# GpSimd's scatters one pass later, the keys' scaling ahead of the first addition, and the state's second scaling ahead of the last three additions

## The reference

```python
mixed = conv4(einsum('bth,ch->btc', layernorm(x), qkv_w))   # causal, one filter per channel
q, k, v = split(mixed, 3)
def step(S, inp):                     # scan over the tokens, S is 128 x 128 for each head
    S = S * alpha_t
    kv = k_t @ S
    S = S + outer(k_t, (v_t - kv) * beta_t)
    return S, q_t @ S                 # o_t
out = (o * rsqrt(mean(o**2) + eps) * norm_w * silu(z)) @ out_w.T
x = x + out
logits = layernorm(x) @ W_router + b_router       # the best 2 of 8 experts
x = x + sum over the 2 experts of w_e * (relu(xn @ W1[e] + b1[e]) @ W2[e] + b2[e])
```

## Time and profile before

| what | us |
|---|---|
| median of 3 runs | 1395.7 (1393.51 to 1396.22) |
| the profiled execution: its time | 1399.73 |
| the profiled execution: its span | 1397.9 |
| one pass, from one first scatter to the next (601.62 to 668.67) | 67.05 |
| busy in the span: PE, DVE, ACT, POOL | 1199.9, 1164.4, 832.0, 707.9 |

### The profile page before, as it was taken

The page is one execution under the profiler, slowest core; times in us unless marked ns, Lnnn a source line. Parts: engine busy times, 40 slices in busy tenths (PEclk is TensorE's granted clock), DMA queues, the critical chain, the costliest instruction groups (busy, mean ns, idle before and its releaser), DMA issues.

```text
span 1397.9 us, 34191 instructions
## 1 busy us (share of the span) xinstructions
PE 1199.9 (86%) x12203; PEld 944.0 (68%) x12203; DVE 1164.4 (83%) x2531; ACT 832.0 (60%) x2536; POOL 707.9 (51%) x598
## 2 busy tenths in 40 slices
PE   0355999999999999999999999999999989479991
PEld 0233868686868687777777777777777767358881
DVE  6878898989898998989898989897989783578875
ACT  1252666666666666657566666756566655358884
POOL 3151727464555656473828292928192822235552
PEclk9997999999999999999999999999999998789996
DMA  6031212222221222131313141313121223432225
GB/s 208 0 98 32 73 35 73 47 69 62 54 63 53 62 54 64 52 68 48 84 34 91 28 98 25 103 28 88 30 85 43 73 55 98 104 96 78 76 65 181
DMA packets 163176, 97.10 MB, mean 69 GB/s; under 512 B 115623, under 2 KB 148269, under 8 KB 161988
## 3 DMA queue, kind: packets, MB, share of 16 engines
q1 hardware_dynamic: 124932, 82.25, 21.6%
q10 hardware_dynamic: 33536, 4.20, 2.1%
q0 software_dynamic: 4544, 8.47, 1.9%
HBM read 73.31 MB, written 24.61 MB: 70 GB/s over the span
## 4 chain that ended last, share of the span: by engine, by line
DVE 37%; PE 21%; POOL 17%; issue 10%; DMA 9%; SPq 3%; ACT 3%; POOLq 0%; DVEq 0%; ACTq 0%
DVE blkT L1060 9%; POOL kq L637 9%; DVE Y_sb L1056 9%; DMA blkN<-scr_n 4%; PE kx L1553 3%; POOL decay L629 3%; POOL rows_in L609 2%; DVE Gs L1204 2%; POOL kq L620 2%; DMA scr_n<-area 2%; PE rc L1717 2%; SPq L477 2%; DVE blkN L1047 1%; DVE area L1170 1%; DVE Y_sb L1043 1%
## 5 line engine op out<-in xcount | busy, mean ns | idle before, releaser
L637 POOL TENSOR_TENSOR kq<-tapA,area 128x256 f32<-128x256 f32 x256 | 252.0, 998 | 93.6 <-DVE area L1146 92.8
L758 ACT ACTIVATE area<-pj,taps 128x256 f32<-128x256 f32 x256 | 123.1, 481 | 142.7 <-PE pj L1567 136.5
L1056 DVE TENSOR_TENSOR Y_sb<-blkT,blkN 128x4 f32<-128x4 f32 (+18 forms) x304 | 169.5, 558 | 10.5
L609 POOL DMA_INDIRECT rows_in<-rowbuf,dest x64 | 64.6, 1009 | 202.1 <-DVE dest L1132 175.2
L1143 DVE SCALAR_TENSOR_TENSOR tapA<-pj,taps,tapA 128x256 f32<-128x256 f32 x256 | 122.2, 477 | 53.4 <-ACT tapA L758 51.6
L1553 PE MATMUL kx<-kq 128*128 128x128 f32 x1024 | 141.0, 285 | 20.0 <-ACT area L767 9.6
L1553 PEld LDWEIGHTS kx<-kq 128*128 128x128 f32 x1024 | 128.7, 197 | 38.4 <-issue 21.8
L620 POOL TENSOR_TENSOR kq<-kq,area 128x1024 f32<-128x1024 f32 x64 | 151.1, 2362 | 0.0
L1060 DVE TENSOR_REDUCE blkT<-Y_sb 128x2 f32<-128x4 f32 (+18 forms) x304 | 142.4, 469 | 5.2
L758 ACT ACTIVATE tapA<-pj,taps 128x256 f32<-128x256 f32 x256 | 123.0, 480 | 0.0
L1146 DVE SCALAR_TENSOR_TENSOR area<-pj,taps,area 128x256 f32<-128x256 f32 x256 | 121.4, 474 | 0.0
(11 more groups left out here) (307 smaller groups left out, 3613.2 us busy)
## 6 DMA issues: line engine op xcount, KB each, us to landing
area<-scr_alpha SPq DMA_DIRECT2D x32, 512.0 KB, 4.2
area<-scr_acum SPq DMA_DIRECT2D x32, 512.0 KB, 4.0
blkN<-scr_n SPq DMA_DIRECT2D x32, 256.0 KB, 4.4
area<-rows_in SPq DMA_DIRECT2D x39, 130.0 KB, 2.3
scr_n<-area SPq DMA_DIRECT2D x128, 32.0 KB, 1.6
area<-rows_out SPq DMA_DIRECT2D x4, 1024.0 KB, 8.1
rows_in<-rows_in SPq DMA_DIRECT2D x8, 260.0 KB, 3.8
kq<-in_x SPq DMA_DIRECT2D x4, 512.0 KB, 6.2
```

Source lines behind the costliest of these rows:

```text
L637: nc.gpsimd.tensor_tensor(dst[:, n % H, :], tapA[:, n % RING, :], tapB[:, n % RING, :], ALU.add).then_inc(conv_done, 1)
L758: ins = nc.scalar.activation(dst[:, n % RING, :], pj[n % 2][:, k:k + GT], ACT.Copy, scale=taps[:, t, k:k + 1])
L1056: ins = nc.vector.tensor_tensor(p4, bc(blkT[:, r0:, j:].rearrange("p r (o m) -> p r o m", o=1), [128, nr, w, wd]), bc(blkN[:, j:j + w, j:] ...
```

## The change

Three words of `ORDER` move, and `sc` gets another group. `ka.0` moves from behind `first.3` to ahead of `last.0`; on GpSimd that is from behind `last.0` to ahead of it. `sp.1` moves ahead of `last.13`. `sc` moves from the end of a pass to behind `last.15`, and there it scatters the rows of group r - 1 instead of those of r; one call behind the passes does the group that is left over.

```diff
-        ... proj.3 m.0.0 last.0 taps.3 rdiag.0 me.1.0 v.0.1 first.2 proj.4 first.3 ka.0 last.1
+        ... proj.3 m.0.0 ka.0 last.0 taps.3 rdiag.0 me.1.0 v.0.1 first.2 proj.4 first.3 last.1
...
-        ... taps.15 ks.1.1 last.13 rhs.1.0 ...  s2 ac.1 sd.1.0 sp.1 sq.1.1 kd.0.1
+        ... taps.15 ks.1.1 sp.1 last.13 rhs.1.0 ...  s2 ac.1 sd.1.0 sq.1.1 kd.0.1
...
-        ... g.1.0 last.15 kd.1.0 inv.13 ...  st.1.1 xs.1 tj sc
+        ... g.1.0 last.15 sc kd.1.0 inv.13 ...  st.1.1 xs.1 tj
                 for step, *arg in STEPS:
-                    if r is not None:
+                    if step == "sc" and r is not None and r > 0:
+                        route("sc", r - 1, par)
+                    elif step != "sc" and r is not None:
                         route(step, r, par)
...
             stages(NG - 1, None, 0)
+            route("sc", NG - 2, 1)
             for step in ROUTE_ORDER:
                 route(step, NG - 1, 1)
```

More of the change, by code:

```diff
@@ L249, in preln_delta_moe_kernel @@
         ORDER = """
[L250 to L263, removed]
@@ L264, in preln_delta_moe_kernel @@
-            st.1.1 xs.1 tj sc
-            """
+        proj.0 proj.1 taps.0 taps.1 diag.0 first.0 v.0.0 proj.2 m.1.0 taps.2 al.0 first.1 proj.3 m.0.0 ka.0
+        last.0 taps.3 rdiag.0 me.1.0 v.0.1 first.2 proj.4 first.3 last.1 me.0.0 m.1.1 taps.4 proj.5 me.1.1
+        ks.0.0 m.0.1 taps.5 scan.0 first.4 m.1.2 proj.6 me.0.1 rdiag.1 ks.0.1 last.2 last.3 first.5 me.1.2
+        proj.7 m.0.2 m.1.3 al.1 taps.6 diag.1 first.6 taps.7 last.4 proj.8 first.7 kk.0.0 me.0.2 me.1.3 m.0.3
+        last.5 proj.9 last.6 xl.0 rhs.0.0 me.0.3 last.7 sp.0 scan.1 nm.0.0 taps.8 kk.0.1 u.0.0 taps.9 aq.0
@@ new lines, in preln_delta_moe_kernel @@
+        nm.0.1 kk.1.0 first.8 last.8 nm.1.0 kk.1.1 nm.1.1 proj.10 ue.0.0 rhs.0.1 taps.10 o.0.0 first.9 proj.11
+        first.10 proj.12 u.0.1 taps.11 first.11 taps.12 last.9 sd.0.0 proj.13 ktr.0.0 ue.0.1 first.12 xl.1
+        aq.1 last.10 no.0 no.1 sq.0.0 proj.14 taps.13 last.11 st.0.0 ac.0 sd.0.1 taps.14 g.0.0 o.0.1 first.13
+        ka.1 st.0.1 sq.0.1 proj.15 last.12 v.1.0 sm v.1.1 scale.0 bi ks.1.0 kd.0.0 first.14 inv.0 taps.15
+        ks.1.1 sp.1 last.13 rhs.1.0 inv.1 inv.2 last.14 inv.3 inv.4 first.15 rhs.1.1 u.1.0 inv.5 kq.0.0 u.1.1
@@ new lines, in preln_delta_moe_kernel @@
+        ue.1.0 g.0.1 inv.6 ue.1.1 o.1.0 o.1.1 ktr.0.1 sq.1.0 inv.7 s2 ac.1 sd.1.0 sq.1.1 kd.0.1 inv.8 scale.1
+        inv.9 inv.10 at.0.0 inv.11 ktr.1.0 inv.12 g.1.0 last.15 sc kd.1.0 inv.13 rms.0 inv.14 sd.1.1 ktr.1.1
+        kd.1.1 rms.1 gn.0.0 kq.0.1 gn.0.1 gt.0.0 inv.15 at.0.1 z.0.0 inv.16 gt.0.1 gte.0.0 nr g.1.1 xt inv.17
+        gte.0.1 z.0.1 zt.0.0 xe lg out.0 gn.1.0 zt.0.1 inv.18 rk gn.1.1 gt.1.0 inv.19 gt.1.1 x2.0 inv.20
+        gte.1.0 inv.21 kq.1.0 gte.1.1 pf out.1 zg.0.0 z.1.0 tp zt.1.0 zg.0.1 ps st.1.0 z.1.1 zt.1.1 zg.1.0
@@ L266, in preln_delta_moe_kernel @@
+        zg.1.1 xs.0 x2.1 to at.1.0 kq.1.1 at.1.1 ti st.1.1 xs.1 tj
+        """
         STEPS = [(name, *map(int, arg)) for name, *arg in (word.split(".") for word in ORDER.split())]
```

## The result

| what | before | after |
|---|---|---|
| median of the runs, us | 1395.96 (1393.51 to 1397.96, 4 runs) | 1416.53 (1415.26 to 1417.77, 4 runs) |
| the profiled execution, us | 1399.73 | 1417.77 |
| one pass, mean of 13, us | 67.70 | 68.84 |
| from the end of `zg.1.1` to the start of the inverse (the seam), pass 7, us | 33.05 | 32.06 |
| the same, mean of the 13 seams into passes 2 to 14, us | 33.82 | 32.76 |

The change makes the kernel slower: ratio 1.0148, interval 1.0129 to 1.0167, +20.6 us. (A ratio is estimated from all the runs of both kernels, so the last digits need not be those of the quotient of the two medians.)

The account below looks back on a forecast made before the run. TensorE bounds a pass's first half, GpSimd close behind, and VectorE the second. Costs of 32.8 + 3.6 + 4.5 less 9.5 us gave +31.4: 1431.1 profiled, median 4.0 lower, 1427 us; range 1403 to 1443.

Parts of the forecast that it names:

- rival 3: Half of the hold: ka.0 falls where VectorE reads PSUM, or moved sp.1 wins about 1 us; about 1409 us; chance 0.17.
- Scatters cost nothing: Behind last.15, in GpSimd's idle time: scatters land before nr starts and do not disturb VectorE; 0 us, bound under 0.1 a pass.
- The freed seam: Seam between passes, without scatters: 0.73 us gained at each of 13 seams, 9.5 us, with 0.4 and 1.5 as bounds.
- The shorter scan: First half of a pass: scan.0 falls from 3.84 to near 2.28 us, in VectorE's slack and partly inside the 0.73.
- `diag.0`'s hold: End of a pass, behind nr: diag.0 holds VectorE's 351-element inverse product for 1.32 us at 13 ends.
- `ka.0`'s hold: End of a pass, behind diag.0: ka.0 holds VectorE's next inverse product for 1.2 us at 13 ends; bounds 0 and 2.4.
- the three further ends: Ends of the opening pass, pass 0 and pass 14: only ka.0 is new there, 3 x 1.2 = 3.6 us.
- `sp.1` ahead of the additions: Start of the inverse: sp.1 ahead of last.13 costs 0.3 us in 15 passes, 4.5 us; bounds -1.0 and +1.0 a pass.
- The sum: Whole kernel: 32.8 + 3.6 + 4.5 us of holds less 9.5 us at the seams, +31.4 us.
- rival 1: Seam: it pays more than it costs, all 4.9 us a pass could come off; faster, about 1373 us; chance 0.08.
- rival 2: Inverse: the two products do not hold VectorE on its path, only the gain is left; 1386 us; chance 0.05.
- rival 4: End of a pass: no VectorE turn between diag.0 and ka.0, 1.2 us more in 13 passes; about 1443 us; chance 0.10.

Follow-up runs that it names:

- sc_alone: The changed kernel with ka.0 and sp.1 back at their old places, so only the scatters move: 1425.91 against 1421.59 us for the kernel before, ratio 1.0039.
- sp_back: The changed kernel with sp.1 alone back at its old place: 1443.83 against 1421.59 us for the kernel before, ratio 1.0153.
- the held pair: `held` (1404.43 us) and the same kernel with sp.1 back behind last.14 (1407.62 us, ratio 0.9904 to the kernel before), run in one batch.
- held: The changed kernel with diag.0, and ka.0 queued behind it, waiting for the previous pass's last zg.1.1: 1404.43 against 1421.59 us for the kernel before, ratio 0.9876.
- extra_product: The kernel before with diag.0's product done once more behind nr in passes 1 to 13: 1417.38 against 1400.23 us, ratio 1.0128.
- extra_memset: The kernel before with two memsets of diag.0's buffer behind nr in passes 1 to 13: 1398.40 against 1400.23 us, ratio 0.9995.

## Why the prediction was right or wrong

The direction, the mechanism and the places were right, and the time came inside the range. The size was too large by half, +31.4 us for the +20.6 measured. The 1416.53 us lie just below the 1418 to 1436 that I gave my own forecast, and nearer to rival 3's 1409 than to my 1427; it is the room left for rival 3 that put them inside the range.

- **Scatters cost nothing.** Right, as far as the runs show. `nr` waits for `rs` as before, and `sc_alone` has at most 0.2 us a pass beyond `diag.0`'s hold and the seam.
- **The freed seam, 0.73 us.** About right for the seams at full clock: 0.67 (33.43 to 32.76 on average; 0.99 in pass 7 alone). The prediction had no term for the two seams of the kernel before at a lower clock, which the changed kernel does not have: another 5 us in the profiled execution. The shorter scan adds nothing that shows. It takes 2.28 us in the changed kernel and 2.79 in `sc_alone`, as in pass 1 of the kernel before (2.78), and the seams of `sc_alone` are no longer for it (32.53).
- **`diag.0`'s hold, 1.32 us.** Right: 1.33 in the row, 1.27 a pass by experiment, and 17.15 us for 13 of them made on purpose.
- **`ka.0`'s hold, 1.2 us.** Slightly over-sized: 1.01 in the row. The product of 450 elements, 0.63 us long, ends 0.48 us behind `ka.0` (673.93 against 673.45): the first 0.15 us of its record pass while it is held, and 2.37 - 1.14 left that out. At 13 ends of passes that is 2.5 us. At the three further ends (3.6 us) the rows give 3.9: 1.47 and 1.02 on the same product in the opening pass and pass 0, and 1.41 on the one of 351 elements in pass 14, where no `diag.0` goes ahead of `ka.0`.
- **`sp.1` ahead of the additions, +0.3 us.** Wrong, and probably in its sign. (Its own working, 2.4 less 2.0, makes 0.4.) The loss at the start of the inverse is 2.0 us in pass 7 of both kernels; the mean of 13 passes is 1.86 us before and 1.68 after. With `sp.1` back it is 1.91 in `sp_back`, and in the held pair 1.85 against 1.71, with 3.2 us between their medians. So it is nearer to -0.2 a pass than to +0.3. This is the largest error: 4.5 us booked, and some 2.7 more to the other side.
- **The sum.** By the measured terms 13 x (1.33 + 1.01) = 30.4, 3.9 for the further ends, -0.18 x 15 = -2.7 for `sp.1`, and -13 x 1.06 = -13.8 for the seams with their lower clock: 17.8 us. The profiled executions differ by 18.0, the medians by 20.6. The kernel before may have had less of the lower clock in other executions; only the profiled ones show where it fell.

The rivals: the seam does pay (rival 1), but 0.7 to 1.1 us a pass and not 4.9; TensorE is busy for 32.41 of the 32.90 us that are left of the first half. `held` has the seam without the holds and wins 1.2%, not the 4.6% of 64 us. The products do hold VectorE (against rival 2). There is a turn between the two (against rival 4): the 1.86 us product ended at 671.24, 2.2 us ahead of `ka.0`'s end. Rival 3's 1409 is the nearest time, but its mechanism is hardly what happened: both holds came at their places, and of its win of 1 us by `sp.1` some 0.2 may be there.

## What to carry to other kernels

Where two engines share a way into memory, an instruction that is let go early is not free even on an engine with 13 us of idle: ask which instructions of the neighbour it runs beside, and what that neighbour is worth in that stretch. A wait can be the gain: the same change with one wait more was 1.2% faster instead of 1.5% slower. And a share of the chain (GpSimd's 17%, then 5%) says where the chain walked, not what can be won there.

## What the runs showed of the hardware

- GpSimd's memset holds nothing (0.9995, products of 0.53 us), where a product of the same 1.9 us holds one for 1.33 us. A hold doesn't show as idle time; it is inside the recorded length of the instruction, so two passes have to be compared by the lengths of the same instruction.
- The two engines take turns: of two GpSimd products in a row, the second waits for the VectorE product that was held by the first (its record is 2.64 us for 2.37).
- The scatters, issued in the middle of a pass, land sooner than those issued at the seam: median 2.4 us against 4.0 in the earlier trace rows. The changed kernel's line of scatters:

```profile
L610 POOL DMA_INDIRECT rows_in<-rowbuf,dest x64: 966/1026/1548, 309.6 to 1243.2; - x64
...
DMA to landing us min/median/max: 2.3/2.4/5.0
```

- Between 150 and 1100 us the granted clock of the kernel before fell only in two seams, each time behind a short idle of TensorE (every kernel here has further stretches at the lower clock outside of that time). Windows of the kernel before (the columns of the earlier trace rows):

```profile
943.00:944.00 1.00, 0.40 (x3) 0.10 (x1) 0.61 (x2) 0.57 (x2) 0.98 (x2) 1.00 0.77 259
...
946.00:948.00 2.00, 2.00 (x15) 0.75 (x8) 2.00 (x5) 1.79 (x5) 2.00 (x2) 0.55 0.07 23
...
1080.00:1082.00 2.00, 0.87 (x35) 0.80 (x36) 1.01 (x3) 0.79 (x2) 1.98 (x2) 1.00 0.80 244
...
1084.00:1086.00 2.00, 2.00 (x6) 0.74 (x5) 2.00 (x2) 0.78 (x3) 2.00 (x2) 0.50 0.04 8
```

  TensorE is busy for 0.40 of 1 us and 0.87 of 2 us, and then, from 946 and from 1082 us, the granted clock goes to 0.50, which is 1.2 GHz, for about 4 us; the seam is 2.3 and 2.8 us longer than the mean of the others. Between 150 and 1100 us the profiled executions of the changed kernel and of all those made from it (nine in all) have no such stretch; the three with the scatters at the seam (before, `extra_product`, `extra_memset`) have two, one and one. That suggests a second, small benefit of moving the scatters, but no run was made for it.
